# The first context chunk prepared in the third q chunk, and high and low parts stored side by side

## The chip, the cores and the metric

The kernel runs on one core of a Trainium2 chip. The metric is the device time of one execution in microseconds (us); lower is better.

## The reference, cut to what matters

Two batches of 1024 tokens `x` (512 wide) attend to 2048 context tokens each, with 16 heads of 64. Then a quantised feed-forward product follows.

```python
lat = layer_norm(layernorm(x), ln_lat_g, ln_lat_b)
ctx = layer_norm(context, ln_ctx_g, ln_ctx_b)
q = (lat @ Wq)                       # 16 heads of 64
k, v = split(ctx @ Wkv)
k = apply_rope(k, cos, sin)
attn = softmax(clip(q @ k.T * 64**-0.5, -11, 11))
x = x + tanh(g_xattn) * ((attn @ v) @ Wo + bo)
y = layernorm(x)
x = x + tanh(g_ffn) * (int8(y) @ int8(rhs)) * scales
```

## The kernel before

All products are float32 products made of three fast ones: each operand is split into a high part (rounded to the engine's fast format) and a low part (the rest), and high x high, high x low and low x high are summed (`split_product`, L237). The work has three stages: projections (L248), attention (L995) and output (L1242). The order on every engine is written out by hand; engines wait for each other by semaphores alone. All loads and stores named here are issued by SP in its program order, some by ACT.

**Projections, q part.** The 2048 latent tokens are taken in four chunks n = 0 to 3 of 512 tokens. For each chunk TensorE (PE) makes eight groups m = 0 to 7 of 128 q columns; a group is 12 matmuls (3 terms x 4 slices of the 512-long sum) into one of four PSUM banks (L940 to L954). Groups are counted g = 8n + m. ACT copies the bank to `q_hi` (L675), DVE takes the rest into `q_lo` (L849), SP stores each of the two parts to `q_scr` in DRAM as 128 rows of 2 KB (`store_q`, L449). There are four slots for `q_hi` and `q_lo`: ACT waits before group g until the stores of g - 4 have landed (L674). PE waits before group g for the `q_lo` of g - 4 (L945), which frees the bank. Between groups, the engines prepare what comes later, each piece at a hand-picked (n, m): measuring, normalising and turning the next chunk, splitting its tokens into `tok_hi` and `tok_lo` (`tok_split`, L819), the column maxima of `rhs` (`rhs_column`, L787) and its scales.

**First context chunk.** Context is taken in eight chunks of 512 tokens. It comes from DRAM twice: by rows, for mean and deviation of each token (`load_rows` L396, `measure_rows` L760, `sqrt_rows` L621, `invert_rows` L774), and already transposed, by columns, for the product (`load_columns`, L405). The statistics go through DRAM to become rows that every partition holds: ACT stores them (`store_first_stats`, L640), and reads them back broadcast (`spread_first_stats`, L644). Then DVE centres and scales the columns (`normalise_columns`, L778), ACT applies gain and bias (`affine_columns`, L625), and DVE makes `tok_hi` and `tok_lo`. For chunk 0 this lies between q groups: rows are measured at (2, 5), inverted at (2, 6), stored at (2, 7), spread at (3, 0), normalised at (3, 2), given gain and bias at (3, 4) and split at (3, 5).

**Context part.** In a chunk PE alternates between four k quads (2 x 12 matmuls each, banks 2 and 3) and four v tiles (banks 0 and 1) (L959). ACT copies k to `k_raw` (L712) and v to `v_out` (L721); DVE rotates k and splits it into `k_hi` (L893) and `k_lo` (L895); SP stores each part in two halves to `k_scr` (`store_k`, L515), 128 rows of 2 KB each, and v to `v_scr`. PE waits before k quad j for the copy of quad j - 1 (L966). While chunk c is in work, chunk c + 1 is prepared; ACT begins chunk c with `sqrt_rows(c + 1)` (L701), ahead of its copies, and DVE with `measure_rows(c + 1)` (L875).

**Attention.** Sixteen pairs of heads run after each other. Before a pair, `load_pair` (L97) brings k (eight loads), q and v from DRAM; pair 0 is loaded during the last context chunk, pair n + 2 once the values of pair n are done.

## Time and profile before

| | us |
|---|---|
| median of three runs | 1474.84 (1472.64 to 1475.39) |
| the profiled execution, its own time | 1474.27 |
| its span, first to last instruction | 1472.5 |
| q part and first context chunk's preparation | 0 to 119.87 |
| context part | 119.87 to about 470 |
| attention | about 472 to about 1350 |
| output | to 1472.5 |

The page of the profile gives busy time of each engine. PE is TensorE, PEld its weight loads, DVE is VectorE, ACT is ScalarE, SP issues DMAs. In a timeline each line has the start, the time that the merged instructions take, engine, line of the kernel, operation, tile written and tiles read, and how many instructions were merged; a bracket gives the idle time of the engine just before and what ended it. In a view by windows each engine has its busy time in the stretch, then come the granted clock of TensorE as a share of 2.4 GHz, the busy share of the DMA engines, and GB/s.

### The profile page before, as it was taken

How to read it: one execution, taken by the hardware profiler on the slowest of the kernel's cores; microseconds unless marked ns; L12 is line 12 of the kernel's file. 1: busy time of each engine (PE TensorE's matmuls, PEld its weight loads, DVE VectorE, ACT ScalarE, POOL GpSimd, SP SyncE). 2: the span in 40 equal slices, each digit the busy share in tenths (PEclk: the TensorE clock that was granted, in tenths of full speed). 3: DMA queues.
4: the chain of work that ended last, by engine and by line, in shares of the span. 5: the costliest groups of instructions: out<-in, count | busy, mean ns of one | idle time of the engine just before them, and what ended most of it. 6: DMA issues, size and time to landing. Idle time of an engine off the chain costs nothing. (4 is left out here: it accounts for less than half of the span.)

```text
span 1472.5 us, 22437 instructions
## 1 busy us (share of the span) xinstructions
PE 1444.5 (98%) x7930; PEld 873.5 (59%) x7938; DVE 1267.8 (86%) x1112; ACT 705.3 (48%) x821; POOL 101.9 (7%) x66
## 2 busy tenths in 40 slices
PE   8998999999999999999999999999999999999997
PEld 7877888888887444444444444444444444444774
DVE  6747888887764999999999999999999999996987
ACT  4422222222232656656556565565655656654342
POOL 0400000000000000000000000000000000001775
PEclk9998999999999999999999999999999999999998
DMA  8796777668667354551551551451452452303552
GB/s 277 264 295 214 250 242 269 206 231 268 217 202 251 91 122 166 137 128 28 133 129 39 127 129 37 122 129 40 119 129 53 105 129 59 101 16 94 158 164 86
DMA packets 156991, 219.22 MB, mean 149 GB/s; under 512 B 39696, under 2 KB 89872, under 8 KB 149776
## 3 DMA queue, kind: packets, MB, share of 16 engines
q1 hardware_dynamic: 152816, 212.55, 49.4%
q10 hardware_dynamic: 4128, 6.04, 1.2%
q8 instruction: 29, 0.48, 0.1%
q14 instruction: 18, 0.15, 0.0%
HBM read 133.70 MB, written 84.84 MB: 148 GB/s over the span
## 5 line engine op out<-in xcount | busy, mean ns | idle before, releaser
L1167 ACT ACTIVATE prob<-score_ps 128x1024 f32<-128x1024 f32 x512 | 483.2, 1031 | 199.3 <-PE score_ps L1114 199.2
L1126 PE MATMUL value_ps<-prob,v_st 128*64 128x512 f32 x2048 | 467.7, 598 | 1.2 <-DVE prob L1209 1.2
L1225 DVE TENSOR_TENSOR prob_sum<-prob_sum,prob 128x2048 f32<-128x2048 f32 x192 | 440.1, 2292 | 13.5
L1114 PE MATMUL score_ps<-q_st,k_st 64*128 64x512 f32 x3072 | 395.4, 403 | 2.1 <-PEq L112 2.1
L1114 PEld LDWEIGHTS score_ps<-q_st,k_st 64*128 64x128 f32 x3072 | 272.7, 185 | 173.1 <-issue 105.6
L1209 DVE TENSOR_SCALAR prob<-prob 128x4096 f32<-128x4096 f32 x128 | 292.6, 2286 | 42.4 <-ACT prob L1167 40.2
L1126 PEld LDWEIGHTS value_ps<-prob,v_st 128*64 128x64 f32 x2048 | 135.6, 136 | 267.8 <-issue 265.3
L882 DVE TENSOR_TENSOR k_cos<-k_raw,rope 128x1024 f32<-128x1024 f32 x32 | 39.2, 1224 | 64.1 <-ACT k_raw L712 64.1
L1534 POOL MEMSET unround<- 128x1 f32 x1 | 0.1, 99 | 1278.1 <-POOLq L122 1278.1
L712 ACT ACTIVATE k_raw<-proj_ps 128x1024 f32<-128x1024 f32 x31 | 31.9, 1029 | 111.9 <-PE proj_ps L245 111.9
L721 ACT ACTIVATE v_out<-proj_ps 128x1024 f32<-128x1024 f32 x31 | 31.9, 1030 | 110.1 <-PE proj_ps L245 110.1
L1221 DVE TENSOR_TENSOR prob_sum<-prob 128x2048 f32<-128x2048 f32 x32 | 73.4, 2292 | 1.8
L245 PE MATMUL proj_ps<-tok_hi,wkv_hi 128*128 128x512 f32 x248 | 66.7, 391 | 2.5 <-DVE q_lo L849 2.5
L245 PE MATMUL proj_ps<-tok_hi,wkv_lo 128*128 128x512 f32 x248 | 67.1, 393 | 0.0
L245 PE MATMUL proj_ps<-tok_lo,wkv_hi 128*128 128x512 f32 x248 | 66.8, 392 | 0.0
L245 PE MATMUL proj_ps<-wkv_hi,tok_hi 128*128 128x512 f32 x248 | 66.3, 389 | 0.0
L245 PE MATMUL proj_ps<-wkv_hi,tok_lo 128*128 128x512 f32 x248 | 66.3, 389 | 0.0
L245 PE MATMUL proj_ps<-wkv_lo,tok_hi 128*128 128x512 f32 x248 | 66.3, 389 | 0.0
L1180 ACT ACTIVATE sum_row<-sum_ps 128x512 f32<-128x512 f32 x32 | 19.2, 599 | 94.1 <-PE sum_ps L1138 94.1
L245 PEld LDWEIGHTS proj_ps<-tok_hi,wkv_hi 128*128 128x128 f32 x248 | 46.5, 188 | 12.7 <-issue 3.1
L245 PEld LDWEIGHTS proj_ps<-tok_hi,wkv_lo 128*128 128x128 f32 x248 | 47.1, 190 | 9.9
L245 PEld LDWEIGHTS proj_ps<-tok_lo,wkv_hi 128*128 128x128 f32 x248 | 47.1, 190 | 9.9
(125 smaller groups left out, 1317.8 us busy)
## 6 DMA issues: line engine op xcount, KB each, us to landing
k_st<-k_scr SPq DMA_DIRECT2D x128, 256.0 KB, 6.2
k_scr<-k_hi SPq DMA_DIRECT2D x64, 256.0 KB, 2.9
v_scr<-v_out SPq DMA_DIRECT2D x32, 512.0 KB, 3.7
k_scr<-k_lo SPq DMA_DIRECT2D x64, 256.0 KB, 4.3
q_st<-q_scr SPq DMA_DIRECT2D x16, 1024.0 KB, 11.1
v_st<-v_scr SPq DMA_DIRECT2D x16, 1024.0 KB, 13.7
q_scr<-q_hi SPq DMA_DIRECT2D x32, 256.0 KB, 5.4
q_scr<-q_lo SPq DMA_DIRECT2D x32, 256.0 KB, 5.5
```

The costliest lines, as they stand in the source:

```text
L245: last = pe.matmul(acc, s, m, start=(n == 0), stop=(n == len(terms) - 1))
L712: act.activation(k_raw[:, j % 2, :, :], banks(what, j, order), ACT.Copy).then_inc(k_copied, 1)
L721: act.activation(v_out[:, j, :], banks(what, j, order), ACT.Copy).then_inc(v_copied, 1)
L882: last = dve.tensor_tensor(made[:, :, :], k_raw[:, s, :, :], rope[:, slot, f:f + 1, :].broadcast_to((P, 2, CH)), ALU.mult)
L1114: last = pe.matmul(score_ps[:, u % BANKS, a, :], k_st[slot][rows, k_part, s * P:(s + 1) * P], q_st[slot][rows, q_part, cols], start=(t == ...
L1126: last = pe.matmul(value_ps[rows, :], v_st[slot][:, s, rows], prob[:, b % 2, i, a * CH:(a + 1) * CH], start=(s == 0), stop=(s == STEPS - 1))
L1167: act.activation(prob[:, b % 2, u % BATCH_UNITS, :], score_ps[:, u % BANKS, :, :], ACT.Exp, scale=SCALE).then_inc(exped, 1)
L1180: act.activation(late.sum_row[:, :], sum_ps[:, :], ACT.Copy).then_inc(late.sum_copied, 1)
L1209: dve.tensor_scalar(tile, tile, CLIP_LOW, CLIP_HIGH, ALU.max, ALU.min).then_inc(clipped, 1)
L1221: dve.tensor_tensor(total, halves[0], halves[1], ALU.add).then_inc(added, 1)
L1225: dve.tensor_tensor(total, total, halves[j], ALU.add).then_inc(added, 1)
L1534: pool.memset(unround[:, :], -ROUND).then_inc(unround_set, 1)
```

## The change

Two things change.

**Storage.** `q_hi` and `q_lo` become one tile `q_parts` with the two parts of a group side by side, `k_hi` and `k_lo` become `k_parts`. The scratch tensors get the same order: 512 values of the high part, then 512 of the low part, so a row of a store is 4 KB. `store_q` waits for the low part and issues one store instead of two (32 instead of 64 in all); `store_k` waits for the low part and issues two stores instead of four. A pair's k is loaded by four DMAs instead of eight, with rows of 16 KB. The score matmuls index the tiles accordingly; their number and shapes stay. The thresholds of the semaphores follow.

**Order.** The preparation of context chunk 0 moves ahead:

| step | engine | before (n, m) | after (n, m) |
|---|---|---|---|
| load rows of chunk 0 | SP | (2, 0) | (1, 5) |
| measure rows | DVE | (2, 5) | (2, 1) |
| square root | ACT | (2, 6) | (2, 2) |
| invert | DVE | (2, 6) | (2, 3) |
| load columns of chunk 0 | SP | (2, 5) | (2, 3) |
| store statistics | ACT | (2, 7) | (2, 4) |
| spread statistics | ACT | (3, 0) | (2, 7) |
| normalise columns | DVE | (3, 2) | (3, 1) |
| gain and bias | ACT | (3, 4) | (3, 3) |
| split tokens | DVE | (3, 5) | (3, 4) |
| rope tables of chunk 0 | SP | (3, 2) | (3, 1) |
| load rows of chunk 1 | SP | (3, 0) | (3, 5) |
| load columns of chunk 1 | SP | (3, 1) | after (3, 7) |
| rope tables of chunk 1 | SP | (3, 4) | after (3, 7) |

```diff
@@ -56,9 +56,9 @@
-    q_scr = nc.dram_tensor("q_scr", (BATCH, INNER, 2, NQ), F32, kind="Internal").ap()
-
-    k_scr = nc.dram_tensor("k_scr", (BATCH, QUADS, 4, P, NS), F32, kind="Internal").ap()
+    q_scr = nc.dram_tensor("q_scr", (BATCH, INNER, NQ // CH, 2, CH), F32, kind="Internal").ap()
+
+    k_scr = nc.dram_tensor("k_scr", (BATCH, QUADS, 2, P, NS // CH, 2, CH), F32, kind="Internal").ap()
     v_scr = nc.dram_tensor("v_scr", (BATCH * NS, INNER), F32, kind="Internal").ap()
...
@@ -97,14 +97,12 @@
             for a in range(2):
-                for part in range(2):
-                    for half in range(2):
-                        row = a * DHEAD + half * HALF
-                        sp.dma_start(k_st[slot][row:row + HALF, part, :].bitcast(F32),
-                                     k_scr[b, quad, 2 * part + half, bass.ds((j + a) * HALF, HALF), :]
-                                     ).then_inc(kqv_in[slot], 16)
-            sp.dma_start(q_st[slot][:, :, :].bitcast(F32),
-                         q_scr[b, bass.ds(pair * P, P), :, :]).then_inc(kqv_in[slot], 16)
+                for half in range(2):
+                    row = a * DHEAD + half * HALF
+                    sp.dma_start(k_st[slot][row:row + HALF, :, :, :].bitcast(F32),
+                                 k_scr[b, quad, half, bass.ds((j + a) * HALF, HALF), :, :, :]).then_inc(kqv_in[slot], 16)
+            sp.dma_start(q_st[slot][:, :, :, :].bitcast(F32),
+                         q_scr[b, bass.ds(pair * P, P), :, :, :]).then_inc(kqv_in[slot], 16)
             sp.dma_start(v_st[slot][:, :, :],
@@ -269,15 +267,13 @@
         wq_lo = lsb("wq_lo", [P, 2, KT, WQ_COLS], F32R)
-        q_hi = lsb("q_hi", [P, QSLOT, CH], F32R)
-        q_lo = lsb("q_lo", [P, QSLOT, CH], F32R)
+        q_parts = lsb("q_parts", [P, QSLOT, 2, CH], F32R)
     v_out = sb("v_out", [P, CT, INNER])
...
     k_rot = sb("k_rot", [P, 2, 2, CH])
-    k_hi = sb("k_hi", [P, 2, 2, CH], F32R)
-    k_lo = sb("k_lo", [P, 2, 2, CH], F32R)
+    k_parts = sb("k_parts", [P, 2, 2, 2, CH], F32R)
     wkv_lo = sb("wkv_lo", [P, KT, 2 * INNER], F32R)
@@ -450,10 +446,9 @@
             b, c0 = n * CH // NQ, n * CH % NQ
-            for part, made, t in ((0, q_hi_made, q_hi), (1, q_lo_made, q_lo)):
-                sp.wait_ge(made, g + 1)
-                sp.dma_start(q_scr[b, m * P:(m + 1) * P, part, c0:c0 + CH],
-                             t[:, s, :].bitcast(F32)).then_inc(q_stored[s], 16)
+            sp.wait_ge(q_lo_made, g + 1)
+            sp.dma_start(q_scr[b, m * P:(m + 1) * P, c0 // CH, :, :], q_parts[:, s, :, :].bitcast(F32)
+                         ).then_inc(q_stored[s], 16)
@@ -492,10 +487,12 @@
                     load_chunk(n + 2, n % 2, chunk_rows(n + 2))
-                if m == 0 and n + 2 >= QCH:
-                    load_rows(n + 2 - QCH, (n + 2 - QCH) * CH)
-                if (n, m) in ((2, 5), (3, 1)):
-                    load_columns(n - 2, n - 2, (n - 2) * CH)
+                if (n, m) == (1, 5):
+                    load_rows(0, 0)
+                if (n, m) == (2, 3):
+                    load_columns(0, 0, 0)
+                if (n, m) == (3, 5):
+                    load_rows(1, CH)
                 if (n, m) in ((0, 3), (1, 0), (1, 4), (2, 0)):
@@ -505,37 +502,35 @@
                     load_stage(4 + m // 2)
-                if n == 3 and m in (2, 4):
-                    load_rope(m // 2 - 1, m // 2 - 1, (m // 2 - 1) * CH)
+                if (n, m) == (3, 1):
+                    load_rope(0, 0, 0)
...
-        def store_k(c, quad, b, s0, part):
-            s = quad % 2
-            made, t = ((k_hi_made, k_hi), (k_lo_made, k_lo))[part]
-            sp.wait_ge(made, QUADS * c + quad + 1)
+        def store_k(c, quad, b, s):
+            i = quad % 2
+            sp.wait_ge(k_lo_made, QUADS * c + quad + 1)
             for half in range(2):
-                sp.dma_start(k_scr[b, quad, 2 * part + half, :, bass.ds(s0, CH)],
-                             t[:, s, half, :].bitcast(F32)).then_inc(k_stored[s], 16)
+                sp.dma_start(k_scr[b, quad, half, :, bass.ds(s, 1), :, :], k_parts[:, i, half, :, :].bitcast(F32)
+                             ).then_inc(k_stored[i], 16)
...
             wo_row, rhs_row = [[sp.snap((c + i) * size) for i in (1, 2)] for size in (P, RHS_ROWS)]
-            b, s0, tok0 = sp.snap(c // 4), sp.snap((c % 4) * CH), sp.snap(c * CH)
+            b, s, tok0 = sp.snap(c // 4), sp.snap(c % 4), sp.snap(c * CH)
             for what, j in order:
...
                 if what == "k":
-                    store_k(c, j, b, s0, 0)
                     if order[order.index(("k", j)) + 1][0] == "k":
-                        store_k(c, j, b, s0, 1)
+                        store_k(c, j, b, s)
                     continue
...
                 if before[0] == "k":
-                    store_k(c, before[1], b, s0, 1)
+                    store_k(c, before[1], b, s)
                 if j == 0 and following:
@@ -547,26 +542,28 @@
+        load_columns(1, 1, CH)
+        load_rope(1, 1, CH)
         with sp.Fori(0, CCH // 2 - 1) as i:
...
         for s in range(QSLOT):
-            sp.wait_ge(q_stored[s], 32 * QCH * MT // QSLOT)
+            sp.wait_ge(q_stored[s], 16 * QCH * MT // QSLOT)
         for s in range(CT):
...
         for s in range(2):
-            sp.wait_ge(k_stored[s], 64 * (CCH - 2) * QUADS // 2)
+            sp.wait_ge(k_stored[s], 32 * (CCH - 2) * QUADS // 2)
         sp.wait_ge(turned, KT * QCH)
...
         for s in range(QSLOT):
-            sp.wait_ge(q_stored[s], 32 * QCH * MT // QSLOT)
+            sp.wait_ge(q_stored[s], 16 * QCH * MT // QSLOT)
         for s in range(2):
-            sp.wait_ge(k_stored[s], 64 * CCH * QUADS // 2)
+            sp.wait_ge(k_stored[s], 32 * CCH * QUADS // 2)
@@ -671,13 +668,13 @@
                 if g >= QSLOT:
-                    act.wait_ge(q_stored[g % QSLOT], 32 * (g // QSLOT))
-                act.activation(q_hi[:, g % QSLOT, :], proj_ps[:, g % 4, :], ACT.Copy).then_inc(q_hi_made, 1)
+                    act.wait_ge(q_stored[g % QSLOT], 16 * (g // QSLOT))
+                act.activation(q_parts[:, g % QSLOT, 0, :], proj_ps[:, g % 4, :], ACT.Copy).then_inc(q_hi_made, 1)
                 if (n, m) == (0, 0):
...
                     sqrt(n + 2)
-                if m == 6 and n + 2 == QCH:
+                if (n, m) == (2, 2):
                     sqrt_rows(0, 0)
@@ -685,11 +682,11 @@
                     load_inverses()
+                if (n, m) == (2, 4):
+                    store_first_stats()
                 if (n, m) == (2, 7):
-                    store_first_stats()
-                if (n, m) == (3, 0):
                     spread_first_stats()
-                if (n, m) == (3, 4):
+                if (n, m) == (3, 3):
                     affine_columns(0, 0)
...
@@ -846,8 +843,8 @@
                 dve.wait_ge(q_hi_made, g + 1)
-                dve.tensor_tensor(q_lo[:, g % QSLOT, :], proj_ps[:, g % 4, :],
-                                  q_hi[:, g % QSLOT, :].bitcast(F32), ALU.subtract).then_inc(q_lo_made, 1)
+                dve.tensor_tensor(q_parts[:, g % QSLOT, 1, :], proj_ps[:, g % 4, :],
+                                  q_parts[:, g % QSLOT, 0, :].bitcast(F32), ALU.subtract).then_inc(q_lo_made, 1)
                 if (n, m) == (0, 0):
@@ -861,13 +858,13 @@
                     rhs_integers(0)
-                if m == 5 and n + 2 == QCH:
+                if (n, m) == (2, 1):
                     measure_rows(0, 0)
-                if m == 6 and n + 2 == QCH:
+                if (n, m) == (2, 3):
                     invert_rows(0, 0)
-                if m == 2 and n + 1 == QCH:
+                if (n, m) == (3, 1):
                     normalise_columns(0, 0)
-                if m == (4, 3, 3, 5)[n]:
+                if m == (4, 3, 3, 4)[n]:
                     tok_split(n + 1, slot, tok if n + 1 < QCH else ctok[0])
@@ -889,10 +886,10 @@
                 if not (isinstance(c, int) and c == 0 and j < 2):
-                    dve.wait_ge(k_stored[s], 32 * (g - s))
-                dve.tensor_copy(k_hi[:, s, :, :], k_rot[:, s, :, :]).then_inc(k_hi_made, 1)
+                    dve.wait_ge(k_stored[s], 16 * (g - s))
+                dve.tensor_copy(k_parts[:, s, :, 0, :], k_rot[:, s, :, :]).then_inc(k_hi_made, 1)
                 dve.wait_ge(k_hi_made, g + 1)
-                dve.tensor_tensor(k_lo[:, s, :, :], k_rot[:, s, :, :], k_hi[:, s, :, :].bitcast(F32),
+                dve.tensor_tensor(k_parts[:, s, :, 1, :], k_rot[:, s, :, :], k_parts[:, s, :, 0, :].bitcast(F32),
                                   ALU.subtract).then_inc(k_lo_made, 1)
...
@@ -1111,8 +1109,8 @@
                         rows = slice(a * DHEAD, (a + 1) * DHEAD)
-                        last = pe.matmul(score_ps[:, u % BANKS, a, :], k_st[slot][rows, k_part, s * P:(s + 1) * P],
-                                         q_st[slot][rows, q_part, cols], start=(t == 0), stop=(t == len(TERMS) - 1))
+                        last = pe.matmul(score_ps[:, u % BANKS, a, :], k_st[slot][rows, s // KEYS, k_part, keys],
+                                         q_st[slot][rows, half, q_part, :], start=(t == 0), stop=(t == len(TERMS) - 1))
                 last.then_inc(scored, 1)
```

## Rows read from the trace of the kernel before

**Rows 1.** The page, part 1: busy time, share of the span and instructions.

```profile
PE 1444.5 (98%) x7930; PEld 873.5 (59%) x7938; DVE 1267.8 (86%) x1112; ACT 705.3 (48%) x821; POOL 101.9 (7%) x66
```

**Rows 2.** By windows, around the start of the context part.

```profile
100.00:150.00 50.00, 42.70 (x169) 33.92 (x168) 33.97 (x44) 13.04 (x19) 0.00 (x0) 0.90 0.74 253
150.00:200.00 50.00, 50.00 (x223) 41.40 (x222) 42.41 (x52) 15.83 (x19) 0.00 (x0) 1.00 0.69 232
```

**Rows 3.** Waits of PE: line, waited for, us in total, times, longest.

```profile
PE proj_ps L245 <- DVE q_lo L849: 7.3, 3, 3.9
```

**Rows 4.** Timeline of PE, 84 to 128 us.

```profile
95.81 1.07 PE L245 MATMUL proj_ps<-tok_hi,wq_hi 128*128 128x512 f32 x4
...
98.53 1.07 PE L245 MATMUL proj_ps<-tok_hi,wq_hi 128*128 128x512 f32 x4
...
102.33 1.19 PE L245 MATMUL proj_ps<-tok_hi,wq_hi 128*128 128x512 f32 x4 [0.92 <-DVE q_lo L849]
...
111.94 2.08 PE L245 MATMUL proj_ps<-tok_hi,wq_hi 128*128 128x512 f32 x4 [3.87 <-DVE q_lo L849]
...
119.87 1.44 PE L245 MATMUL proj_ps<-tok_hi,wkv_hi 128*128 128x512 f32 x4 [2.51 <-DVE q_lo L849]
...
127.00 1.07 PE L245 MATMUL proj_ps<-wkv_hi,tok_hi 128*128 128x512 f32 x4
```

**Rows 5.** By windows, inside the last q group.

```profile
112.00:114.00 2.00, 2.00 (x5) 1.62 (x6) 0.49 (x1) 2.00 (x4) 0.00 (x0) 0.50 0.94 309
```

**Rows 6.** Timeline of DVE and ACT: from the statistics to the split tokens.

```profile
89.57 0.40 ACTq L642 DMA_DIRECT2D stat_scr<-stat  x1
...
99.82 1.04 ACTq L648 DMA_DIRECT2D tok<-stat_scr  x2
...
106.67 2.29 DVE L783 TENSOR_TENSOR w_stage<-w_stage,tok 128x2048 f32<-128x2048 f32 x1 [3.79 <-DMA tok<-stat_scr]
...
111.33 2.93 ACT L628 ACTIVATE w_stage<-w_stage,gains 128x512 f32<-128x512 f32 x4 [8.30 <-DVE w_stage L785]
...
116.69 2.29 DVE L827 TENSOR_TENSOR tok_lo<-w_stage,tok_hi 128x2048 fp32r<-128x2048 f32 x1
```

**Rows 7.** Timeline, groups (1, 5) to (2, 3), where steps are put in.

```profile
64.55 0.33 SPq L455 DMA_DIRECT2D q_scr<-q_lo  x1
...
70.44 1.88 DVE L849 TENSOR_TENSOR q_lo<-proj_ps,q_hi 128x512 fp32r<-128x512 f32 x3
...
79.78 0.69 DVE L789 TENSOR_REDUCE rhs_amax<-rhs_col 128x1 f32<-128x512 f32 x1 [5.99 <-DMA rhs_col<-rhs_t_dram]
```

**Rows 8.** Timeline, context chunk 0: preparation of chunk 1.

```profile
122.20 2.46 DVE L764 BATCH_NORM_STATS2 moments<-raw 128x6 f32<-128x512 f32 x4
...
125.12 0.30 ACT L623 ACTIVATE std<-stat,eps_col 128x4 f32<-128x4 f32 x1 [6.96 <-DVE stat L771]
...
127.29 1.03 ACT L712 ACTIVATE k_raw<-proj_ps 128x1024 f32<-128x1024 f32 x1 [1.87 <-PE proj_ps L245]
...
157.92 2.29 DVE L827 TENSOR_TENSOR tok_lo<-w_stage,tok_hi 128x2048 fp32r<-128x2048 f32 x1
```

**Rows 9.** DMA issues: count, KB each, median us from issue to landing.

```profile
q_scr<-q_lo SPq DMA_DIRECT2D x32, 256.0 KB, 5.5
...
raw<-context_dram SPq DMA_DIRECT2D x8, 1024.0 KB, 7.0
...
tok<-stat_scr ACTq DMA_DIRECT2D x2, 256.0 KB, 5.6
...
scale_scr<-rhs_scales ACTq DMA_DIRECT2D x1, 4.0 KB, 4.8
stat_scr<-stat ACTq DMA_DIRECT2D x1, 4.0 KB, 10.2
```

**Rows 10.** Timeline of DVE, the split of a k quad.

```profile
132.14 0.69 DVE L893 CAST k_hi<-k_rot 128x1024 fp32r<-128x1024 f32 x1
...
132.87 1.23 DVE L895 TENSOR_TENSOR k_lo<-k_rot,k_hi 128x1024 fp32r<-128x1024 f32 x1
```

More of the change, by code:

```diff
@@ L87, in flamingo_kernel @@
             tok = esb("tok", [P, KT, CH])
-        k_st = [sb("k_st0", [P, 2, NS], F32R)]
-        q_st = [sb("q_st0", [P, 2, NQ], F32R)]
+        k_st = [sb("k_st0", [P, NS // CH, 2, CH], F32R)]
+        q_st = [sb("q_st0", [P, NQ // CH, 2, CH], F32R)]
         v_st = [sb("v_st0", [P, STEPS, P])]
@@ L707, in context_chunk @@
                         for s in range(QSLOT):
-                            act.wait_ge(q_stored[s], 32 * QCH * MT // QSLOT)
+                            act.wait_ge(q_stored[s], 16 * QCH * MT // QSLOT)
                     act.wait_ge(k_summed, QUADS * c + j + 1)
@@ L1003, in attention @@
     BANKS = 3
+    KEYS = CH // P
     ADDS = 2 * HALF_BATCHES - 1
-    k_st.append(sb("k_st1", [P, 2, NS], F32R))
-    q_st.append(sb("q_st1", [P, 2, NQ], F32R))
+    k_st.append(sb("k_st1", [P, NS // CH, 2, CH], F32R))
+    q_st.append(sb("q_st1", [P, NQ // CH, 2, CH], F32R))
     v_st.append(sb("v_st1", [P, STEPS, P]))
@@ L1020, in attention @@
     bo_in = sem("bo_in")
-    KQV = 16 * 10
+    KQV = 16 * 6
     TERMS = ((0, 0), (1, 0), (0, 1))
@@ L1105, in scores @@
                 half, s = divmod(u, STEPS)
-                cols = slice(half * CH, (half + 1) * CH)
+                keys = slice(s % KEYS * P, (s % KEYS + 1) * P)
                 if u >= BANKS:
```

## The prediction, made before the changed kernel was run

> **What bounds the kernel now.** I began with the page: PE is busy for 98% of the span and DVE for 86% [rows 1]. So little can be won but where PE stands still or runs at the lower of its two clock levels. The windows show where that is: from 100 to 150 us PE is busy for 42.70 of 50 us and the granted clock is 0.90 on average, from 150 us on it is 50.00 of 50 at full clock [rows 2]. The view of waits names one cause: PE waits three times for a `q_lo` of DVE, 7.3 us in all [rows 3]. The timeline places them: 0.92 us before group (3, 5) at 102.33, 3.87 us before (3, 7) at 111.94, 2.51 us before the first context quad at 119.87 [rows 4].
>
> What would the stretch take undisturbed? Two group starts, 95.81 and 98.53, give 2.72 us for a group of 12 matmuls [rows 4]; (3, 4) would end at 101.25. From there to the end of the first k quad lie five groups, 13.6 us, which gives 114.85; that end is at 127.00 [rows 4]. So **12.15 us** are lost here: 7.3 us by standing still, and the rest by the clock. After the 3.87 us pause PE runs at 0.50, that is at 1.2 instead of 2.4 GHz [rows 5], and (3, 7) takes from 111.94 to about 117.36 (119.87 less the pause of 2.51), 5.42 instead of 2.72 us; the first k quad takes 7.13 us (119.87 to 127.00) instead of 5.44. These two make 4.4 us.
>
> The waits for `q_lo` are not DVE's own slowness. The chain behind them is that of context chunk 0 [rows 6]: ACT issues the store of the statistics at 89.57, waits for its landing until 99.82 and issues the broadcast; while it waits, it copies no q group, which makes the 0.92 us. DVE waits for the broadcast until 106.67, with the next `q_lo` behind it; ACT starts gain and bias at 111.33, DVE ends the split of the tokens at 118.98, and the `q_lo` of (3, 6), on which the first context quad waits, comes after that. From the start of centring, called T here (106.67), to the first context matmul (119.87) there are 13.2 us.
>
> **The order, step by step.** *Rows of chunk 0.* The place (1, 5) comes when SP stores `q_lo` of group 13, at 64.55 [rows 7]. A context load of 1 MB lands after 7.0 us [rows 9]: 71.5, or 74.8 if it took the 10.2 us of the slowest row there. The place of measuring, after `q_lo` of group 17, is at 70.44 + 1.88 = 72.3 [rows 7]. Measuring takes 2.46 us and 2.92 until the square root starts (122.20 to 125.12, [rows 8]), so the statistics are ready for it at 75.2, at worst at 77.7. What stands behind it on DVE is the `q_lo` of group 18, then the maximum of a `rhs` column, which waits for a DMA until 79.78 in any case [rows 7]; SP issues that DMA after one q store instead of two and after no load of rows, so rather at 78 to 79. PE needs these `q_lo` only four groups, 10.88 us, later. Cost: nothing; the wait for the column covers it, and without that cover it would be 2.9 us of DVE inside a 10.88 us slack.
>
> *Statistics.* After the column and `q_lo` of group 19, DVE inverts at about 80.2, and ACT issues the store at (2, 4) at about 80.9, against 89.57. For the landing there are two rows of the same shape on the same queue: 4.8 us for the scales and 10.2 us for the statistics [rows 9]. Ends: 85.7 and 91.1. The spread stands behind the copy of (2, 7), at 88.5 (that group ends 3 x 2.72 before 95.81, at 87.65; the k copy starts 0.3 after its matmuls and takes 1.03 for twice the columns [rows 8], so 0.3 + 0.5). I take the 4.8 us, because the scales' store was also made while q stores went out, and nothing of ACT's queue is ahead of it; then ACT does not wait at all. Between the broadcast's issue and T lay 6.85 us before (99.82 to 106.67, [rows 6]): T = 95.4. It can't be ahead of 94.5, when `q_lo` of (3, 1) is done (95.81 - 2.72 + 0.8 for the copy + 0.63), and is 98.0 with the slow store.
>
> The Trainium skill (DMA: Bandwidth & Descriptors, section on queues, rings and completion order) says that an engine takes turns between the queues packet by packet, so that the small pieces of ACT's store would pass SP's backlog; that favours the 4.8 us. The same rule speaks against the change too: each turn of SP's queue now has rows of 4 KB. That is a rival below.
>
> *Behind T.* The chain of 13.2 us stays, with one `q_lo` more in it: the split is now ahead of `q_lo` of (3, 5) and (3, 6). One `q_lo` is 1.88/3 = 0.63 us [rows 7], so, rounded to 0.6, the first context matmul is at T + 13.8 = 109.2. PE itself gets there at 101.25 + 8.16 = 109.4 if no q group stalls. (3, 6) needs the `q_lo` of (3, 2), which follows centring and scaling: T + 4.66 (106.67 to 111.33, [rows 6]) + 0.65 = 100.7, needed at 103.97; (3, 7) follows 0.63 later with 2.72 more. So the first quad starts at 109.6 (a handoff of 0.2), 111.8 at the late end, instead of 119.87. If PE never pauses for long, the clock stays, and the quad takes 5.44 us: it ends at 115.0 instead of 127.00. **Gain 12.0 us** (late end: 9.8, less up to 2.7 for the clock).
>
> *Chunk 1.* Its rows were loaded at (3, 0) and had been there long before DVE measured them at 122.20 [rows 8]. Now they are issued after `q_lo` of (3, 5), at T + 13.6 = 109.0, and land at 116.0 by 7.0 us. DVE is free by then (its small work on `wo` and `rhs` ends about 113). Measured 118.9 (2.92 later), square root 0.30, and only then does ACT copy the first k quad (1.03, [rows 8]): 120.3. PE wants that bank at 109.6 + 10.88 = 120.5. So this wait is just covered; with a landing of 10.2 us it costs 3.2. I put **0.3 us** into the sum and keep 0 to 3.2. After that chunk 1's chain: its low tokens are made by 160.2 [rows 8], PE needs the tokens at about 165.1 (127.00 + 7 x 5.44), 4.9 us later. It moves ahead by DVE's first rotation, from 128.4 to 120.4, by 8 us, PE by 12: the slack shrinks by 4 and covers this, the more so as low tokens are needed 1.8 us after the high ones. Moved past each other on SP are eight rope issues (those of chunk 0 now ahead of the store of (3, 2): at 0.33 to 0.52 each, by the issues in [rows 6, 7], up to 4.2 us, done at about 99 while DVE still centres) and those of chunk 1, which now come before `store_v`; neither is asked for before 120.
>
> **The storage, step by step.** *q.* 32 stores fewer on SP. The price is in the wait: ACT's copy of group g needs the store of g - 4, which now leaves whole after the low part. Low parts land 5.5 us after issue [rows 9]; the double store takes 5.5 to 7.0 (the 1 MB load, [rows 9]). The copy of g - 4, `q_lo` and issue take about 1.9 us, so 7.4 to 8.9 of 10.88 us: covered, 0. *k.* DVE's writes get a gap of 512 values between the halves. Before there is no such row: the cast takes 0.69 for 1024 values and the subtraction 1.23 [rows 10]. Between these ends, 0 to 0.54 us for each of 32 casts, I take 0.69, since the inner runs stay 512 long; even the other end is 17 us spread over 350 in which DVE is busy for 42.41 of 50 us [rows 2], and on no path that PE waits for. The Trainium skill (VectorE: DVE Perf Modes, on what auto-detection checks) gives the doubled rate when the outermost dimensions are even, which would leave the cast at 0.69; no row has this shape. *End of the context part.* The last quad's high halves leave 1.23 us later, with the low ones [rows 10]; the stage waits for their landing, beside that of the last v copy. Bounds 0 and 1.23, I take **0.4**. *Attention.* Half the k issues, rows of 16 KB: the loads are hidden behind a whole pair on either side, 0; score matmuls keep size and count.
>
> **Sum.** -12.0 + 0.3 + 0.4 = -11.3. The profiled execution took 1474.27 (the median is 1474.84), so 1463.0; I say **1463.2**. Its own range, 1461.5 to 1465.5.
>
> **Rivals.** (A) *The wait moves to the second k quad* (chance 0.18): rows of chunk 1 land late behind q stores and block ACT. For it: ACT takes the square root first, and the margin is 0.2 us. Against: the 7.0 us. It costs up to 3.2 us, and up to 2.7 by the clock: 1466 to 1469. (B) *The statistics land as late as now* (0.13): 10.2 us, T = 98.0, the context starts at 111.8, 2.4 us after (3, 7) ends; with the clock 2.7 more: 1465 to 1468. (C) *The small store queues behind 4 KB rows* (0.04): if the part of 10.2 us that lies above 4.8 doubled and more, to some 17 us, it would land at 98, T = 105, and the context start at 118.8: 1473, no difference. The Trainium skill's rule of turns stands beside this. (D) *Slower: q stores become the beat of the q part* (0.03). Where: ACT's wait for the slot in all 28 groups from the fifth. It decides when issue to landing passes 10.88 - 1.9 = 9.0 us; each four groups then cost the excess. To eat the 11.3 us, it must be 9.0 + 11.3 x 4/28 = 10.6; at 11.5 it would cost 7 x 2.5 = 17.5 us, 6.2 more than is won: 1480. For it: these stores meet loads of 1 MB; against it: 5.5 us [rows 9].
>
> **Numbers.** The forecast has 0.62. The 80% range must take in A and B: 1461.0 to 1469.0. About 0.2% (2.9 us) is what a measurement of this kernel can tell from no change. Forecast, A and B are all faster by more: 0.93; C and the rest near it: 0.04; slower: 0.03.
>
> **What would show it.** Right: no bracket on PE between 84 and 115 us, or one under a microsecond; the first context matmul near 109.6; full clock throughout; `stat_scr` stored near 81 and landed before 88.5; centring near 95.4; the cast of L893 still at 0.69. The k copy of the first quad near 120.3 shows whether A holds: a bracket on PE near 120.5. Wrong: a context start after 112, a granted clock of 0.5 near it, q stores above 9 us to landing, or pauses of PE for `q_lo` in chunks n = 1 and 2, which have none now [rows 3, 4].

## The result, and the profile after

The changed kernel takes **1466.97 us** (median of six runs, 1463.1 to 1469.37) against 1475.01 us before (median of six, one of which took 6938 us; 1474.84 without it). The ratio, which leaves that one run out, is 0.995, with a 95% interval of 0.9933 to 0.9966: 7.4 us won, between 5.0 and 9.9. The forecast was 1463.2, a gain of 11.3; the range held the result, the size was off by a third.

The profiled execution happens to be the slowest of the six, 1469.37 us with a span of 1467.5. The page's part 1 of it, for [rows 1]:

```profile
PE 1443.2 (98%) x7938; PEld 872.8 (59%) x7938; DVE 1268.2 (86%) x1112; ACT 705.2 (48%) x821; POOL 101.9 (7%) x66
```

By windows, the same two stretches as [rows 2] and two short ones around the first context quad:

```profile
100.00:150.00 50.00, 45.60 (x193) 36.93 (x192) 36.87 (x46) 13.95 (x20) 0.00 (x0) 0.97 0.79 249
150.00:200.00 50.00, 50.00 (x223) 41.39 (x222) 42.44 (x51) 14.25 (x17) 0.00 (x0) 1.00 0.71 248
...
114.00:116.00 2.00, 1.37 (x5) 1.17 (x6) 2.00 (x4) 0.00 (x0) 0.00 (x0) 0.87 0.72 248
116.00:118.00 2.00, 2.00 (x6) 1.51 (x6) 1.00 (x3) 0.00 (x0) 0.00 (x0) 0.50 1.09 223
```

PE is busy for 45.60 of 50 us, not 42.70, but not for 50 either, and the clock still falls to 0.50 once. Waits of PE, the row that answers to [rows 3]:

```profile
PE proj_ps L243 <- DVE q_parts L846: 4.4, 2, 2.8
```

Two pauses are left of three. The timeline, with PE, DVE, ACT and SP mixed, shows the chain that answers to [rows 4, 6 and 8]:

```profile
81.74 0.44 ACTq L630 DMA_DIRECT2D scale_scr<-rhs_scales  x1
81.82 0.43 SPq L407 DMA_DIRECT2D w_stage<-context_t_dram  x1
...
82.22 0.76 ACTq L639 DMA_DIRECT2D stat_scr<-stat  x1
...
86.79 0.34 ACTq L635 DMA_DIRECT2D inv_row<-scale_scr  x1
...
90.74 0.88 ACTq L645 DMA_DIRECT2D tok<-stat_scr  x2
...
100.86 2.29 DVE L780 TENSOR_TENSOR w_stage<-w_stage,tok 128x2048 f32<-128x2048 f32 x1 [5.17 <-DMA tok<-stat_scr]
...
105.51 2.93 ACT L625 ACTIVATE w_stage<-w_stage,gains 128x512 f32<-128x512 f32 x4 [5.81 <-DVE w_stage L782]
...
106.13 1.20 PE L243 MATMUL proj_ps<-tok_hi,wq_hi 128*128 128x512 f32 x4 [1.63 <-DVE q_parts L846]
...
114.18 0.43 SPq L398 DMA_DIRECT2D raw<-context_dram  x1
...
114.63 1.32 PE L243 MATMUL proj_ps<-tok_hi,wkv_hi 128*128 128x512 f32 x4 [2.77 <-DVE q_parts L846]
...
120.95 2.47 DVE L761 BATCH_NORM_STATS2 moments<-raw 128x6 f32<-128x512 f32 x4 [3.88 <-DMA raw<-context_dram]
...
121.78 1.07 PE L243 MATMUL proj_ps<-wkv_hi,tok_hi 128*128 128x512 f32 x4
...
125.14 1.03 ACT L709 ACTIVATE k_raw<-proj_ps 128x1024 f32<-128x1024 f32 x1 [0.96 <-DMA q_scr<-q_parts]
...
129.99 0.69 DVE L890 CAST k_parts<-k_rot 128x1024 fp32r<-128x1024 f32 x1
```

The first context matmul comes at 114.63 instead of 119.87, 5.24 us sooner. That is the whole difference of the two spans (1472.5 and 1467.5): the first quad takes 7.15 us (to 121.78) as against 7.13, from there to the first score matmul (466.77) it is 344.99 in both, and attention and output agree within 0.2 us. The stretches behind the first quad thus show nothing of the storage. The DMA issues, with the median time to landing, for [rows 9]:

```profile
q_scr<-q_parts SPq DMA_DIRECT2D x32, 512.0 KB, 6.2
...
tok<-stat_scr ACTq DMA_DIRECT2D x2, 256.0 KB, 8.0
...
inv_row<-scale_scr ACTq DMA_DIRECT2D x1, 256.0 KB, 7.7
...
scale_scr<-rhs_scales ACTq DMA_DIRECT2D x1, 4.0 KB, 5.0
stat_scr<-stat ACTq DMA_DIRECT2D x1, 4.0 KB, 8.5
```

So what is missing lies ahead of the start of centring, T: the store of the statistics landed after 8.5 us, the broadcast left at 90.74 instead of 88.5, and DVE could begin 10.1 us after that, instead of 6.85.

### The profile page after: what moved, and what is told of

The parts are those of the page before. It is cut to its first block and busy times, and to the rows that moved or that the text cites. A ratio compares the mean times of both kernels' runs of the same rounds, so it can differ in the third digit from the quotient of the medians.

```text
span 1467.5 us, 22093 instructions
## 1 busy us (share of the span) xinstructions
PE 1443.2 (98%) x7938; PEld 872.8 (59%) x7938; DVE 1268.2 (86%) x1112; ACT 705.2 (48%) x821; POOL 101.9 (7%) x66
```

## The experiments

Theory 1: the stretch from 64 to 101 us has no DMA time to spare, so what the change moved into it lands late. Theory 2: it is the 4 KB rows on SP's queue that hold up the broadcast on ACT's. A further question was whether another wait lies right behind the one that was removed.

### The order alone

The edit: the kernel before, with every line of the change's order (the table above) and none of its storage.

> The changed order on the old storage (two stores of 2 KB rows per q group, k as before). In the changed kernel the broadcast of the statistics was issued at 90.7 us and centring began at 100.9 us, 5.5 us later than predicted, which is most of what is missing. Theory 1, the stretch is full: the 2 MB of context loads were moved into a stretch where the DMA engines had no room, so everything in it lands later, whatever the rows' length. Then this kernel is about as fast as the changed one, 1466 to 1468, with centring at about 100. Theory 2, turns: the rows of 4 KB on SP's queue hold up the 2 KB rows of the broadcast on ACT's queue. Then centring begins near 95 to 96 here and the kernel takes 1462 to 1464.

Measured: median 1464.86, ratio 0.9934 (0.992 to 0.9948). Its timeline:

```profile
90.83 0.86 ACTq L652 DMA_DIRECT2D tok<-stat_scr  x2
...
99.31 2.29 DVE L787 TENSOR_TENSOR w_stage<-w_stage,tok 128x2048 f32<-128x2048 f32 x1 [4.31 <-DMA tok<-stat_scr]
...
113.09 1.15 PE L245 MATMUL proj_ps<-tok_hi,wkv_hi 128*128 128x512 f32 x4 [2.77 <-DVE q_lo L853]
...
125.36 1.20 PE L245 MATMUL proj_ps<-tok_hi,wkv_hi 128*128 128x512 f32 x4 [1.15 <-ACT k_raw L716]
```

Centring begins at 99.3 with rows of 2 KB too, near theory 1's 100 and far from theory 2's 95 to 96. The order carries all of the gain. The time, though, lies between the two theories' (1466 to 1468 and 1462 to 1464): the median is 2.1 us below the changed kernel's first six runs and 2.7 below those made beside it (1467.55, the changed kernel again). This profile also has what the prediction called rival A: a pause of 1.15 us at the second k quad, behind ACT's copy of the first.

### The storage alone

The edit: the changed kernel, with the order of before.

> The new storage in the old order. Theory 1 (full stretch): no effect beyond 1 us, 1474 to 1476. Theory 2 (turns): the statistics' broadcast, issued at about 100, lands in about 10 us instead of 6.85, and the context part starts 3 us later: 1477 to 1479. In both, the stage change to attention comes at most 1.2 us later after the last v copy, if the last k store matters at all.

Measured: median 1474.97, ratio 1.0007 (0.9999 to 1.0016): at most a little slower than the kernel before, which had a median of 1473.46 beside it. The broadcast left at 100.93 and centring began at 107.88, 6.95 us later, against 6.85 in [rows 6]. Theory 2 wanted some 10 us. The pause at the change to attention was 2.11 us, as before, so the last k store's later start costs nothing. Up to the end of the first k quad this profile is 1.0 us behind the kernel before (127.99 against 127.00). Its span is the same (1472.4 and 1472.5) only because the first scores of attention took 1.1 us less, by a difference in the clock that is not the storage's (granted 1.00 at 472 to 476 us, 0.57 in the kernel before; see the last section).

### Two stores per q group

```diff
-            sp.wait_ge(q_lo_made, g + 1)
-            sp.dma_start(q_scr[b, m * P:(m + 1) * P, c0 // CH, :, :], q_parts[:, s, :, :].bitcast(F32)
-                         ).then_inc(q_stored[s], 16)
+            for part, made in ((0, q_hi_made), (1, q_lo_made)):
+                sp.wait_ge(made, g + 1)
+                sp.dma_start(q_scr[b, m * P:(m + 1) * P, c0 // CH, part, :], q_parts[:, s, part, :].bitcast(F32)
+                             ).then_inc(q_stored[s], 16)
```

> The changed kernel, but each q group is stored in two halves as before, the high part as soon as it is there, into the same places of the new scratch; k keeps its new stores. Theory 1: 1466 to 1468, centring at about 100, since the bytes are the same. Theory 2: 1462 to 1464, centring at 95 to 97. A third reading, that ACT stands still because the whole store of a group leaves only after its low part: ACT's waits for q_scr stores (10.0 us in the changed kernel between 40 and 130 us) fall below 3 us here, and the time by less than 2 us.

Measured: median 1467.08, ratio 0.9951 (0.9938 to 0.9964), as the changed kernel. Centring began at 98.7 and the context part at 112.50, 2 us sooner than in the changed kernel's profile, but the median says that this is no lasting gain. Of theory 2's 95 to 97 nothing is seen. The third reading is out as well: ACT still waited for landings of q stores (15.0 us in eight waits between 40 and 130 us, the longest 5.25), though the high part left at once.

### The changed kernel again

> The changed kernel once more, word for word, beside the others on the same chip. Its six runs so far lie between 1463.1 and 1469.4, the profiled one being the slowest of them; before's lie within 3 us. Both theories: median 1466 to 1468. If the profiled run comes out near 1463, its centring must begin near 95 and the context part near 110, which would show that the spread sits in this one stretch.

Measured: median 1467.55 (1465.48 to 1469.09), ratio 0.9952. Its profiled execution, 1469.09, repeats the other one: centring at 100.89, context at 114.67, 7.17 us for the first quad. No profile near 1463 came up here, so that part of the expectation stays untested by this kernel.

### Without the broadcast

```diff
-                act.dma_start(rows[:, 0, f, :], stat_scr[f:f + 1, :].broadcast_to((P, CH))).then_inc(rows_in[0], 16)
+                act.dma_start(rows[0:16, 0, f, 0:CT], stat_scr[f:f + 1, 0:CT].broadcast_to((16, CT))).then_inc(rows_in[0], 16)
...
+            if isinstance(c, int) and c == 0:
+                spread = [ones[:, 0:1].rearrange("p (a b) -> p a b", a=1).broadcast_to((P, KT, CH))] * 2
```

> The changed kernel without the broadcast of chunk 0's statistics: 16 partitions get 4 values each instead of 128 partitions 512, and centring and scaling of chunk 0 use a tile of ones instead (so chunk 0's tokens are not normalised). This takes away the transfer that landed at 100.8 us. Theory 1 (what is missing of the forecast is this landing alone): centring begins at 95.7, when the q_lo of (3, 1) is done in the changed kernel, the first context matmul comes at 95.7 + 13.8 = 109.5, with no pause before it, and the kernel takes 1462 to 1463.5. Theory 2 (a second limit lies right behind): the pause moves to the second k quad, because ACT copies the first one only after the chunk 1 rows are measured and all q stores have landed (125.1 us in the changed kernel); PE wants that bank at 120.4, so 3 to 5 us come back there, and the time is 1465 to 1468, hardly better than the changed kernel.

Measured: **1461.29** (1460.83 to 1462.72), ratio 0.9916 (0.9903 to 0.9929), 0.7 us below what theory 1 expected. Its timeline around centring and the first context matmuls:

```profile
95.55 2.29 DVE L782 TENSOR_TENSOR w_stage<-w_stage,ones 128x2048 f32<-128x2048 f32 x1 [0.33 <-DMA tok<-stat_scr]
...
109.78 1.17 PE L243 MATMUL proj_ps<-tok_hi,wkv_hi 128*128 128x512 f32 x4 [0.25 <-DVE q_parts L848]
...
119.66 1.03 ACT L709 ACTIVATE k_raw<-proj_ps 128x1024 f32<-128x1024 f32 x1 [0.86 <-DMA q_scr<-q_parts]
```

This is the forecast's own picture: T at 95.55 (said: 95.4), context at 109.78 (109.6), copy of the first quad at 119.66 to 120.7 (120.3), no pause at the second quad, the first quad in 5.55 us. With the landing out of the way, and 512 KB less in the stretch, nothing else stood between the change and its forecast. Theory 2 of this run, a second limit right behind, is refuted for a broadcast that is out of the way; as order_only shows, it is near.

### Half the bytes of six q groups

```diff
-            sp.dma_start(q_scr[b, m * P:(m + 1) * P, c0 // CH, :, :], q_parts[:, s, :, :].bitcast(F32)
+            width = 2 if g < 20 or g > 25 else 1
+            sp.dma_start(q_scr[b, m * P:(m + 1) * P, c0 // CH, 0:width, :], q_parts[:, s, 0:width, :].bitcast(F32)
                          ).then_inc(q_stored[s], 16)
```

> The changed kernel, but the groups (2, 4) to (3, 1) store their high part only (256 KB instead of 512 KB each, rows of 2 KB); the missing parts are filled with other values after the q part. 1.5 MB leave the stretch from 85 to 96 us. If the stretch is short of DMA time, the broadcast lands in 6 to 7 us instead of 10.1 and centring begins at 97 to 98; the kernel gains 2 to 3 us, 1464 to 1465. If the broadcast is slow by itself (one row of DRAM read by 128 partitions), centring stays at 100 to 101 and the time at 1467.

Measured: 1464.19 (1463.65 to 1465.08), ratio 0.9933 (0.9918 to 0.9948). Its timeline, from the broadcast's issue to centring:

```profile
90.88 0.84 ACTq L652 DMA_DIRECT2D tok<-stat_scr  x2
...
96.85 2.29 DVE L787 TENSOR_TENSOR w_stage<-w_stage,tok 128x2048 f32<-128x2048 f32 x1 [1.27 <-DMA tok<-stat_scr]
```

The same broadcast, issued at the same time, is there after 5.97 us instead of 10.1. It is not slow by itself; it waits for DMA time. (Rows of these six stores are 2 KB here, so length and bytes change together. With rows of 2 KB and all the bytes, order_only has 8.48 us and q_two_stores 8.85, so of the 4.1 us no more than 1.3 to 1.6 can be put down to the length; and the last run below, with rows of 4 KB, has 8.50.)

### Less ahead of the broadcast

Order alone, with three transfers moved:

```diff
-                if (n, m) == (3, 5):
+                if (n, m) == (3, 3):
                     load_rows(1, CH)
...
-                if (n, m) == (3, 1):
+                if (n, m) == (3, 4):
                     load_rope(0, 0, 0)
...
-                if (n, m) == (2, 5):
+                if (n, m) == (3, 2):
                     load_inverses()
```

> The new order on the old storage (1464.9 us), with three transfers moved out of the broadcast's way or to where they are needed: the inverses' broadcast (256 KB) from (2, 5) to (3, 2), the rope tables of chunk 0 (512 KB) from (3, 1) to (3, 4), the rows of chunk 1 from (3, 5) forward to (3, 3). Theory 1: centring begins near 97 instead of 99.3, the first context matmul near 111, and the second k quad no longer waits: 1461 to 1463. If ACT's wait for the landing of the last q stores sets that copy and not the rows, its 1.15 us pause at the second k quad stays: 1463 to 1464.

Measured: 1466.31 (1464.29 to 1471.81), ratio 0.9958 (0.9942 to 0.9973): a miss in time (1461 to 1463 was expected) and a hit in the step it aimed at. The profile is of its fastest execution, 1464.29; two of the six took 1470.06 and 1471.81, and why is not known. Its timeline, from centring to the context:

```profile
96.03 2.29 DVE L787 TENSOR_TENSOR w_stage<-w_stage,tok 128x2048 f32<-128x2048 f32 x1 [1.66 <-DMA tok<-stat_scr]
...
110.24 0.63 ACT L658 ACTIVATE raw<-raw 128x512 fp32r<-128x512 f32 x1 [5.66 <-DMA raw<-wo_dram]
...
112.34 1.17 PE L245 MATMUL proj_ps<-tok_hi,wkv_hi 128*128 128x512 f32 x4 [3.00 <-DVE q_lo L853]
```

Centring begins 3.3 us sooner, but from there to the context it is 16.3 us, not 13.8: the 1 MB of chunk 1's rows now goes out ahead of the `wo` piece, ACT waits 5.66 us for that piece with the copy of (3, 6) behind it, and PE for both. One wait took the place of another. The clock stayed at full speed all the same: the first quad takes 5.56 us.

### The statistics sooner

The same, with `invert_rows(0, 0)` on DVE at (2, 2) ahead of the `rhs` column and `store_first_stats()` on ACT at (2, 3) ahead of gain and bias.

> The same, and the chain of the statistics starts sooner: inverted at (2, 2) ahead of the rhs column, stored at (2, 3) ahead of gain and bias, instead of (2, 3) and (2, 4). The store leaves at about 79 instead of 81.4 and may have landed at 88.5, where the spread is placed; then the spread leaves 2 us sooner, and centring begins at 95 to 96: 1460 to 1462. If the landing takes as long as before (9 us) but the q copies behind it get delayed, no gain over the other.

Measured: 1462.84 (1462.19 to 1464.70), ratio 0.9923 (0.9909 to 0.9936). That is 0.8 us above the range expected. The store left at 77.98, the spread at 88.31 as hoped, centring began at 95.50. The `wo` wait was still there, 4.64 us: context at 111.91, and after PE's pause of 1.94 us before it the first quad took 7.14 us.

### The wo piece out of the way

```diff
-                if (n, m) == (3, 5):
+                if (n, m) == (3, 7):
                     wo_high(0)
```

> The kernel before this one that started the statistics sooner (old storage, 1462.8 us), with ACT's rounding of the first wo piece moved from (3, 5) to (3, 7). There it waited 4.6 us for its load and kept the copy of (3, 6) back, so that the first context matmul came 16.4 us after centring began instead of 13.8. If that is the whole reason, the chain is 13.8 again: centring at 95.5, context at 109.5, no pause over 0.5 us, no fall of the clock at the first k quad (5.55 us for it), and 1459.5 to 1460.8. If the rows of chunk 1 or the last q stores then hold the second quad, a pause of 1 to 3 us appears near 120 and the time is 1461 to 1463.

Measured: **1460.98** (1460.41 to 1462.79), ratio 0.9921 (0.9908 to 0.9934), 0.2 us above the range for the case that the piece was the whole reason. By windows, from 100 to 150 us:

```profile
100.00:150.00 50.00, 50.00 (x223) 41.39 (x222) 37.97 (x50) 16.56 (x22) 0.00 (x0) 1.00 0.79 264
```

And in its timeline:

```profile
78.36 0.41 ACTq L646 DMA_DIRECT2D stat_scr<-stat  x1
...
81.04 0.43 SPq L411 DMA_DIRECT2D w_stage<-context_t_dram  x1
...
95.22 2.29 DVE L787 TENSOR_TENSOR w_stage<-w_stage,tok 128x2048 f32<-128x2048 f32 x1 [0.43 <-DMA tok<-stat_scr]
...
109.59 1.07 PE L245 MATMUL proj_ps<-tok_hi,wkv_hi 128*128 128x512 f32 x4
...
115.03 1.07 PE L245 MATMUL proj_ps<-wkv_hi,tok_hi 128*128 128x512 f32 x4
```

PE has no pause in the whole stretch and full clock; the first quad takes 5.44 us. This version is below both kernels, by some 6 us below the changed one, on the old storage.

### The same on the new storage

> The same edits on the new storage. If 4 KB stores cost something only by landing the broadcast later, centring begins 1 to 2 us later than in its twin, and the time is up to 2 us above it. If the storage is neutral, the two agree within 1 us.

Measured: 1461.86 (1461.36 to 1464.81), ratio 0.9926 (0.9914 to 0.9938). Centring began at 97.36, the context at 111.14. So 0.9 us above its twin, with intervals that overlap widely. This pair alone shows no cost. But it is the third in which the new storage is behind, beside the order alone (2.7 us between medians of the same session) and the storage alone (1.5). The means of the three pairs lie 2.9, 1.1 and 0.8 us apart; when the runs are shuffled within each pair, a sum as large comes up in fewer than one of a thousand shuffles. So the new storage most likely costs about one to three microseconds.

### PE kept busy in the pause

```diff
+        pe.wait_ge(affine_made, KT * QCH)
+        for i in range(18):
+            pe.transpose(turn_ps[:, 0, 0:P], ident[:, :], ident[:, :])
         pe.wait_ge(w_hi_made, 6)
```

> The changed kernel, with 18 small transposes (2.9 us by the 0.163 us of those at the start) on PE in the pause of 2.8 us before the first context quad. In the profiles so far the first k quad took 5.55 us or 7.15 us after pauses of the same length, by whether the granted clock fell. If the pause itself makes it fall, the quad takes 5.55 here, the time is 1.6 us lower (1465 to 1466) and the spread of the runs narrower. If the clock falls without a pause, nothing changes: 1466 to 1468.

Measured: 1464.69 (1462.42 to 1467.63), ratio 0.9939 (0.9926 to 0.9953). PE's part of its timeline, with the added transposes first:

```profile
109.88 2.13 PE L955 MATMUL turn_ps<-ident 128*128 128x128 f32 x18
112.82 1.17 PE L243 MATMUL proj_ps<-tok_hi,wkv_hi 128*128 128x512 f32 x4 [0.81 <-DVE q_parts L846]
...
118.36 1.07 PE L243 MATMUL proj_ps<-wkv_hi,tok_hi 128*128 128x512 f32 x4
```

The 18 transposes take 2.13 us instead of 2.9 and leave a pause of 0.81. The quad takes 5.54 us at full clock, and the median is 2.3 us below the changed kernel's first six runs and 2.9 below its repeat. But the spread is no narrower; in this profile centring began at 99.0, 1.9 us sooner than in the other two of the same order and storage, which accounts for most of the gain; and two profiles without the transposes kept the full clock after pauses as long (2.77 us in order_only, 3.00 in less_ahead). So it stays open whether filling the pause keeps the clock up.

## Why the prediction was right or wrong

**Where the time was to be won: right.** All of the gain came from the stretch that [rows 3 and 4] name, and nothing from attention or context. The forecast put the loss there at 12.15 us; best_old, without any pause, starts the context at 109.59 and takes 5.44 us for the quad, the forecast's undisturbed figures.

**The chain behind T: right.** "T + 13.8" was measured as 13.77 (changed kernel), 13.78 (order alone) and 13.77 (half the bytes). It holds as long as `wo` is there in time: 16.3 and 16.4 us where it was not.

**The step that failed is T itself**: 95.4 was said, 100.86 came. It has two terms. The first is "I take the 4.8 us": the store of the statistics took 8.5 us and held the spread back to 90.74, 2.2 us. The prediction had both ends, 4.8 and 10.2, and chose the wrong one, because "nothing of ACT's queue is ahead of it".

The scales' store was, by half a microsecond (81.74). What weighed more was on SP's queue: the columns of chunk 0, 1 MB, issued at 81.82, 0.4 us before the store. The landing times in all thirteen profiles sort by the place of that load:

- In the eight profiles in which the store left that close behind the load it took 7.5 to 9.4 us (q_two_stores 7.5, the changed kernel 8.5, order_only 9.4 among them), while the scales' store, issued just ahead of the load, took 4.0 to 5.6 (7.4 in stats_sooner).
- In the kernel before and in storage_only, where no small store stood ahead on ACT's queue (in the former a broadcast was still out) and the load was 2.7 and 3.1 us ahead, it took 10.2 and 10.1.
- In the three in which it left 2.4 to 2.7 us ahead of the load it took less: 6.3 (stats_sooner), 4.8 (best_old) and 3.9 (best_new).

The packets in the changed kernel's trace fit: the load's move from 84.0 to 88.2 us, those of the scales' store from 83.9 to 84.3, those of the statistics' store from 86.2 to 88.3. No run moved the load alone, so this is a pattern in thirteen profiles and not a test of its own. The Trainium skill (DMA: Bandwidth & Descriptors, section on queues, rings and completion order) has the engines take turns between queues; in none of the ten profiles with the load ahead did this spare ACT's small store the wait.

The second term is "between the broadcast's issue and T lay 6.85 us": it was taken over as if fixed, and was 10.1. half_bytes, with 1.5 MB less, has 5.97. ACT's own queue had something ahead here too, which the prediction left out: the broadcast of the inverses, 256 KB, issued at 86.79 and landed after 7.7 us, at 94.5, when the statistics' broadcast had been out for 3.8 us; in the kernel before it was there at 91.9 (86.17 + 5.7), 8 us ahead of the other. less_ahead, which moves it and the rope tables behind, has 6.38 us against order_only's 8.48; which of the two counts was not separated. The prediction priced the landings one by one and never added up what would be queued around them. The busy share of the DMA engines would not have told it. By windows over the flight of the broadcast, the kernel before (6.85 us) and the changed kernel (10.1 us):

```profile
99.80:106.70 6.90, 5.98 (x27) 4.63 (x26) 1.32 (x3) 2.07 (x4) 0.00 (x0) 1.00 1.00 342
...
90.70:100.90 10.20, 10.20 (x46) 8.45 (x46) 1.43 (x3) 2.39 (x4) 0.00 (x0) 1.00 1.02 342
```

In best_old, with 7.13 us, the share is 1.06.

**What the late T cost.** In the profiled execution the context starts 5.0 us after the forecast's 109.6, and the first quad takes 1.7 us more than 5.44 at the lower clock. With the forecast's 1463.0 that makes 1469.7, against 1469.37. The median execution, 2.4 us faster, has no profile.

**Rival B** (statistics late, 1465 to 1468) is thus what happened, and its price was about right, 1466.97; it had 0.13. It was thought of as the store alone; the broadcast's own landing weighed more.

**The consequences of a late T**: by the prediction's terms (T + 5.3 against 103.97) group (3, 6) is held up when T passes 98.7. It was, by 1.63 us, and 2.77 us before the context are what remains of the chain. The second pause was 2.75 to 2.78 us in all four profiles with T from 98.7 to 100.9 and nothing put into it.

**Rival A** is real but small: a pause at the second k quad of 1.15 us in order_only, 0.59 in half_bytes and 0.37 in kept_busy, none in the others. In the changed kernel the first quad ran at the lower clock, which left ACT more time for its copy. The chain of the prediction for it missed one wait: ACT's first k copy also waits for all q stores to have landed (L708 of the kernel before), and this came last in most profiles, after the rows of chunk 1 (125.14 - 0.96 = 124.18).

**The storage, 0.4 in the sum: right for the parts that it priced, but a small cost was missed.** The cast stayed at 0.69 [rows 10], 129.99 in the timeline above, and the 0.4 us for the last k store was not needed. "Covered, 0" for the q stores' wait did not hold: ACT waits for them 10.0 us in four waits between 40 and 130 in the changed kernel, 8.7 in order_only, 4.8 in storage_only and not at all in the kernel before. So both the crowded stretch and the 4 KB stores bring such waits. They reach PE only through T, which is 1.2 us later in storage_only than in the kernel before (107.88 and 106.67), 1.6 later in the changed kernel than in order_only and 2.1 later in best_new than in best_old (though kept_busy, on the new storage too, has 99.0). With the medians this makes a cost of about one to three microseconds likely; through which wait it comes was not separated. **Rivals C and D** did not come: no q store became the beat, and rows of 2 KB land nearly as late.

## What to carry to other kernels

Moving a chain of small transfers to an earlier place moves it to other traffic: before pricing it by its old landing times, count the bytes that will be queued around it there, on both queues. A busy share near 1.0 does not give the price: it went with 6.0 as with 10.1 us for the same broadcast. Issue the small transfer on which the chain hangs ahead of the next large load, on whatever queue that is; in these runs that went with 3.9 to 6.3 us instead of 7.5 to 10.2. When a wait is removed, follow each engine's program order behind it, for the next load that it waits for (here `wo`) takes the gain at once.

## What the runs showed that I had not expected

Equal pauses of PE cost differently from one execution to the next. After a pause of 2.77 us before the context the first quad took 7.15 us in the changed kernel (granted clock 0.50 at 116 to 118 us) and 5.52 in order_only, which stayed at full clock. less_ahead stayed there after 3.00 us (5.56 for the quad), and stats_sooner fell after 1.94 (7.14; granted clock 0.55 at 112 to 114 us). So the length of the pause alone does not decide it. After the pause of 2.10 us before attention, the time from the first score matmul to the first value matmul was 8.27 us in the kernel before and in both profiles of the changed kernel (8.28 in q_two_stores), 7.15 or 7.16 in eight others, order_only and storage_only among them, and 7.88 in no_broadcast. T too moved, between 99.0 and 100.9, in the same order and storage. These two are what I can name of the spread of 6 us and more between runs of one kernel (6.3 in the changed kernel, 7.5 in less_ahead); whether they make up the whole of it is open. A difference below 3 us between two profiles says little without the stretch in which it arises.

DMA engines can be busy and move little: from 88 to 92 us in the changed kernel their share is 1.05 at 206 GB/s, four microseconds later 1.02 at 404 GB/s. Halving the q stores did not change it (1.07 at 208). It is neither the column load, whose last packets move at 88.2, nor the broadcasts: in the changed kernel's trace 0.92 of the engines' time from 88 to 92 us goes into the 4 KB packets of the q stores, 328 ns each, against 161 ns in the four microseconds behind. Why they are slow there is open. By windows, the changed kernel:

```profile
88.00:92.00 4.00, 4.00 (x19) 3.31 (x18) 1.25 (x2) 0.60 (x1) 0.00 (x0) 1.00 1.05 206
92.00:96.00 4.00, 4.00 (x20) 3.30 (x19) 1.38 (x2) 1.20 (x2) 0.00 (x0) 1.00 1.02 404
```
